# Graph attention pair: which engine forms and empties the pairwise differences in the statistics pass

## The reference

```python
D = jnp.abs(x[:, :, None, :] - x[:, None, :, :])
h = jnp.einsum('bijc,oc->bijo', D, W1) + b1
m = jnp.mean(h, axis=(0, 1, 2))
v = jnp.mean((h - m) ** 2, axis=(0, 1, 2))
h = (h - m) / jnp.sqrt(v + EPS) * g1 + be1
h = _leaky(h)
s = jnp.einsum('bijo,uo->biju', h, W2)[..., 0] + b2[0]
s = jnp.where(A_init > 0, s, NEG)
A = jax.nn.softmax(s, axis=-1)
y = jnp.einsum('bij,bjc->bic', A, x)
```

## Time and profile before

| | us |
|---|---|
| median of 3 runs | 2515.38 |
| lowest to highest | 2508.46 to 2524.46 |
| the profiled execution | 2519.5 |
| its span | 2517.8 |
| ScalarE busy | 2262.2 |
| VectorE busy | 2116.5 |
| TensorE busy (products) | 2052.3 |

### The profile page before, as it was taken

How to read it: one execution, slowest core, us unless ns; L and a number is a source line. 1 busy time by engine, 2 the same in 40 slices (tenths; PEclk the granted TensorE clock), 3 DMA queues, 4 the chain that set the end, 5 groups by cost and what they waited for, 6 DMA issues and landing times.

```text
span 2517.8 us, 36169 instructions
## 1 busy us (share of the span) xinstructions
PE 2052.3 (82%) x12997; PEld 837.5 (33%) x12997; DVE 2116.5 (84%) x2590; ACT 2262.2 (90%) x3505; POOL 61.7 (2%) x58
## 2 busy tenths in 40 slices
PE   4777766888888888888888888887888888888866
PEld 3555542323232322333232333231222222222236
DVE  4888866999999999999999999998878888788845
ACT  4999976999999999999999999996989899889965
POOL 0000000000000000000000000000000001000000
PEclk8999977999999999999999999998999999899978
DMA  3111113444444444444444444447988888888932
GB/s 112 39 44 40 39 47 125 179 161 171 177 173 166 167 171 178 172 170 176 165 172 171 173 171 168 170 162 272 330 308 320 314 314 316 292 314 320 336 114 67
DMA packets 230505, 470.52 MB, mean 187 GB/s; under 512 B 53496, under 2 KB 144312, under 8 KB 213944
## 3 DMA queue, kind: packets, MB, share of 16 engines
q1 hardware_dynamic: 229264, 467.84, 50.6%
q10 hardware_dynamic: 1064, 0.36, 0.1%
HBM read 254.19 MB, written 213.91 MB: 186 GB/s over the span
## 4 chain that ended last, share of the span: by engine, by line
ACT 25%; PE 24%; issue 17%; DVE 14%; DMA 11%; SPq 7%; POOL 2%; ACTq 0%; DVEq 0%; POOLq 0%
PE banks L899 11%; ACT banks L649 10%; DVE diff L1263 6%; DMA ring_scores<-sring 5%; ACT hcopy L646 5%; ACT habs L646 5%; DMA ub<-ring_scores 4%; DVE ring L1116 4%; PE banks L810 2%; SPq L441 2%; POOL ub L502 2%; ACT diff L634 2%; SPq L421 2%; DVE diff L1277 2%; PE banks L914 2%
## 5 line engine op out<-in xcount | busy, mean ns | idle before, releaser
L899 PE MATMUL banks<-diff,w1t 128*64 128x512 f32 x5136 | 1233.5, 611 | 192.8 <-ACT banks L649 142.1
L1263 DVE TENSOR_TENSOR diff<-ring 128x2048 f32<-128x2048 f32 x352 | 802.8, 2288 | 116.3 <-PE banks L899 116.3
L899 PEld LDWEIGHTS banks<-diff,w1t 128*64 128x64 f32 x5136 | 345.2, 138 | 938.7 <-issue 857.3
L649 ACT ACTIVATE banks<-banks,par 128x1024 f32<-128x1024 f32 x512 | 559.2, 1092 | 7.4 <-PE banks L899 4.8
L1277 DVE TENSOR_SCALAR diff<-diff 128x2048 int32<-128x2048 int32 x354 | 415.4, 1219 | 0.0
L1391 DVE TENSOR_TENSOR diff<-ring 128x2048 f32<-128x2048 f32 x128 | 292.7, 2287 | 47.6 <-PE banks L899 47.6
L634 ACT ACTIVATE diff<-banks 128x2048 f32<-128x2048 f32 x128 | 240.3, 1878 | 12.4 <-PE banks L914 12.4
L646 ACT ACTIVATE hcopy<-banks 128x1024 f32<-128x1024 f32 x192 | 197.0, 1026 | 18.4 <-PE banks L899 18.1
L646 ACT ACTIVATE habs<-banks 128x1024 f32<-128x1024 f32 x192 | 197.0, 1026 | 18.4 <-PE banks L899 18.1
L670 ACT ACTIVATE habs<-banks,par 128x1024 f32<-128x1024 f32 x128 | 153.4, 1198 | 46.6 <-PE banks L899 46.6
L914 PE MATMUL banks<-pick,yt 32*128 32x256 f32 x2560 | 184.8, 403 | 10.7 <-DMA yt<-xrows 10.7
(11 more groups left out here) (214 smaller groups left out, 1974.7 us busy)
## 6 DMA issues: line engine op xcount, KB each, us to landing
diff<-kept_two SPq DMA_DIRECT2D x86, 1024.0 KB, 6.8
kept_two<-hcopy SPq DMA_DIRECT2D x128, 512.0 KB, 2.6
kept_two<-habs SPq DMA_DIRECT2D x128, 512.0 KB, 2.6
hcopy<-kept_two SPq DMA_DIRECT2D x42, 1024.0 KB, 6.6
kept_one<-hcopy SPq DMA_DIRECT2D x64, 512.0 KB, 2.6
kept_one<-habs SPq DMA_DIRECT2D x64, 512.0 KB, 2.6
hcopy<-kept_one SPq DMA_DIRECT2D x64, 512.0 KB, 7.5
habs<-kept_one SPq DMA_DIRECT2D x64, 512.0 KB, 7.7
```

The costliest lines, as they stand in the source:

```text
L649: nc.scalar.activation(h, h, ACT.Square, bias=par[:, 53:54], accum_out=column(SQUARES + c)).then_inc(sq_done, 1)
L899: last = nc.tensor.matmul(dst[half * O:(half + 1) * O, bank * BANK:(bank + 1) * BANK], w1t[:, :], src[:, m * BANK:(m + 1) * BANK], start=T ...
L1263: v.tensor_tensor(shaped(diff[:, c % ND, :]), xj, xi_, ALU.subtract).then_inc(sub_done, 1)
```

## The change

All eight rectangle chunks of a graph are made by selection on TensorE. `ORDER` now puts them on the even places, and the diagonal chunks on the odd ones. The even places are emptied in turn: places 0, 4, 8, 12 by ScalarE (`abs_even`, with the sum), places 2, 6, 10, 14 by VectorE, which clears the sign bit while it reads `dps` and writes `diff` (`absolute_of_picked`, `abs_odd`). Selection r serves place 2r, is issued behind the projection of place 2r - 3, and waits for the emptying before. VectorE issues, per four places, the subtractions of 4q+1 and 4q+3, then the absolute values of 4q+1, 4q+2 (out of PSUM) and 4q+3. The x blocks per graph grow from 2 x 5 to 2 x 8. The second selection of the first graph stands before the first projection.

```diff
-    ORDER = [(0, 0), (4, 0), (4, 1), (1, 0), (5, 0), (5, 1), (2, 0), (6, 0), (6, 1), (3, 0), (7, 0), (7, 1),
-             (0, 1), (1, 1), (2, 1), (3, 1)]
-    ON_PE = [(0, 0), (1, 0), (2, 0), (3, 0), (0, 1)]
+    ORDER = [(0, 0), (4, 0), (0, 1), (4, 1), (1, 0), (5, 0), (1, 1), (5, 1),
+             (2, 0), (6, 0), (2, 1), (6, 1), (3, 0), (7, 0), (3, 1), (7, 1)]
-    NP, NR = len(ON_PE), len(REDONE)
+    NP, NR = 2 * RECTS, len(REDONE)
...
-            def absolute(b, j):
-
-                n = b * NP + pe_before(j)
-                act.wait_ge(pd_ready, n + 1)
-                if b or j >= ND:
+            def absolute(b, q):
+
+                j = 4 * q
+                act.wait_ge(pd_ready, b * NP + 2 * q + 1)
+                if b or q:
                     act.wait_ge(h_ready, in_order(b, j) - ND + 1)
...
+                nc.scalar.activation(diff[:, in_order(b, j) % ND, :], dps, ACT.Abs,
+                                     accum_out=column(EVENS + b * NR + q)).then_inc(abs_even, 1)
...
                     sum_h(b, j)
-                    if j + 3 in PE_AT:
-                        absolute(b, j + 3)
-                    if j + 3 == CHUNKS and b + 1 < B:
+                    if j % 4 == 1 and j + 3 < CHUNKS:
+                        absolute(b, (j + 3) // 4)
+                    elif j % 4 == 1 and b + 1 < B:
                         absolute(b + 1, 0)
...
-            def pick_differences(b, j):
+            def pick_differences(b, r):
+
+                k, tp = ORDER[2 * r]
+                if r == 0:
                     pe.wait_ge(blk_loaded[b % 2], 256 * (b // 2 + 1))
-                if n:
-                    pe.wait_ge(abs_pe, n)
-                e = 2 * pe_before(j)
+                if r % 2:
+                    pe.wait_ge(abs_even, b * RECTS + r // 2 + 1)
+                elif b or r:
+                    pe.wait_ge(abs_odd, b * RECTS + r // 2)
+                e = 2 * (RECTS * tp + k)
...
+            pick_differences(0, 1)
             pe.wait_ge(shift_ready, 1)
             for b in range(B):
                 for j in range(CHUNKS):
...
+                    if j % 4 == 0:
+                        pe.wait_ge(abs_even, b * RECTS + j // 4 + 1)
+                    elif j % 4 == 2:
+                        pe.wait_ge(abs_odd, b * RECTS + j // 4 + 1)
                     else:
-                        stat_chunk(in_order(b, j), False, b * (CHUNKS - NP) + dve_before(j) + 1)
-                    if j + 3 in PE_AT:
-                        pick_differences(b, j + 3)
-                    if j + 3 == CHUNKS and b + 1 < B:
-                        pick_differences(b + 1, 0)
+                        pe.wait_ge(abs_dve, b * PAIRS + j // 2 + 1)
+                    stat_chunk(in_order(b, j))
+                    if j % 2 and j + 3 < CHUNKS:
+                        pick_differences(b, (j + 3) // 2)
+                    elif j % 2 and b + 1 < B:
+                        pick_differences(b + 1, (j + 3 - CHUNKS) // 2)
...
+            def absolute_of_picked(b, q):
+
+                j = 4 * q + 2
+                dve.wait_ge(pd_ready, b * NP + 2 * q + 2)
+                if b or q:
+                    dve.wait_ge(h_ready, in_order(b, j) - ND + 1)
+                v.tensor_scalar(diff[:, in_order(b, j) % ND, :].bitcast(I32), dps.bitcast(I32), ABS_BITS, None,
+                                ALU.bitwise_and).then_inc(abs_odd, 1)
...
             for b in range(B):
-                if b:
-                    differences_between(b, 1, 3)
-                differences_between(b, 4, 6)
-                differences_between(b, 7, 9)
-                differences_between(b, 10, 12)
-                differences_between(b, 13, 16)
+                for q in range(RECTS):
+                    z = b * PAIRS + 2 * q + 1
+                    subtract(b, 4 * q + 1)
+                    subtract(b, 4 * q + 3)
+                    absolute(in_order(b, 4 * q + 1), z)
...
+                    absolute_of_picked(b, q)
+                    absolute(in_order(b, 4 * q + 3), z + 1)
```

More of the change, by code:

```diff
@@ L48, in gnn_pair_kernel @@
     BLK = 16
-    ORDER = [(0, 0), (4, 0), (4, 1), (1, 0), (5, 0), (5, 1), (2, 0), (6, 0), (6, 1), (3, 0), (7, 0), (7, 1),
-             (0, 1), (1, 1), (2, 1), (3, 1)]
-    ON_PE = [(0, 0), (1, 0), (2, 0), (3, 0), (0, 1)]
+    ORDER = [(0, 0), (4, 0), (0, 1), (4, 1), (1, 0), (5, 0), (1, 1), (5, 1),
+             (2, 0), (6, 0), (2, 1), (6, 1), (3, 0), (7, 0), (3, 1), (7, 1)]
     REDONE = [(0, 0), (1, 0), (2, 0), (3, 0)]
-    NP, NR = len(ON_PE), len(REDONE)
+    NP, NR = 2 * RECTS, len(REDONE)
     NK = CHUNKS - NR
     KB = 8
-    PE_AT = [j for j, c in enumerate(ORDER) if c in ON_PE]
     STEPS = (0, 4, 1, 5, 2, 6, 3, 7)
@@ L229, in gnn_pair_kernel @@
         pd_ready = sem("pd_ready")
-        abs_pe = sem("abs_pe")
+        abs_even = sem("abs_even")
+        abs_odd = sem("abs_odd")
         abs_dve = sem("abs_dve")
@@ L309, in kept_before @@
             return sum(c not in REDONE for c in ORDER[:j])
[L311 to L317, removed]
         block = ctx.enter_context(nc.Block())
@@ L901, in project @@
                 return last
-            def pick_differences(b, j):
-                n = b * NP + pe_before(j)
-                if pe_before(j) == 0:
+            def pick_differences(b, r):
+                k, tp = ORDER[2 * r]
+                if r == 0:
                     pe.wait_ge(blk_loaded[b % 2], 256 * (b // 2 + 1))
-                if n:
-                    pe.wait_ge(abs_pe, n)
-                e = 2 * pe_before(j)
+                if r % 2:
[3 more added lines that the diff above has]
+                e = 2 * (RECTS * tp + k)
                 for s in range(2):
@@ L917, in pick_differences, with stat_chunk @@
                 last.then_inc(pd_ready, 1)
-            def stat_chunk(c, by_pe, count):
-                pe.wait_ge(abs_pe if by_pe else abs_dve, count)
+            def stat_chunk(c):
                 if c >= 2:
@@ L932, in _ @@
                 for j in range(CHUNKS):
-                    if j in PE_AT:
-                        stat_chunk(in_order(b, j), True, b * NP + pe_before(j) + 1)
-                    else:
-                        stat_chunk(in_order(b, j), False, b * (CHUNKS - NP) + dve_before(j) + 1)
-                    if j + 3 in PE_AT:
-                        pick_differences(b, j + 3)
-                    if j + 3 == CHUNKS and b + 1 < B:
-                        pick_differences(b + 1, 0)
+                    if j % 4 == 0:
+                        pe.wait_ge(abs_even, b * RECTS + j // 4 + 1)
+                    elif j % 4 == 2:
+                        pe.wait_ge(abs_odd, b * RECTS + j // 4 + 1)
+                    else:
+                        pe.wait_ge(abs_dve, b * PAIRS + j // 2 + 1)
[4 more added lines that the diff above has]
+                        pick_differences(b + 1, (j + 3 - CHUNKS) // 2)
             for j in range(2):
-                stat_chunk(B * CHUNKS + j, False, B * (CHUNKS - NP) + j + 1)
+                pe.wait_ge(abs_dve, B * PAIRS + j + 1)
+                stat_chunk(B * CHUNKS + j)
             pe.wait_ge(st_small, 2)
@@ L1295, in _ @@
                 v.tensor_copy(agg[:, 1, half * O:(half + 1) * O], w1t[:, :])
[L1296 to L1301, removed]
-            for b in range(B):
-                if b:
-                    differences_between(b, 1, 3)
-                differences_between(b, 4, 6)
-                differences_between(b, 7, 9)
-                differences_between(b, 10, 12)
-                differences_between(b, 13, 16)
+            for b in range(B):
+                for q in range(RECTS):
[3 more added lines that the diff above has]
+                    absolute(in_order(b, 4 * q + 1), z)
+                    if b == 0 and q == 0:
+                        dve.wait_ge(abs_even, 1)
+                        v.tensor_scalar(par[:, 52:53], yt[:, SUMS + EVENS:SUMS + EVENS + 1], -1.0 / CH, None,
+                                        ALU.mult).then_inc(shift_sum, 1)
+                        dve.wait_ge(shift_half, 1)
+                        v.tensor_copy(par[:, 53:54], ps[3][:, 0:1]).then_inc(shift_ready, 1)
+                    absolute_of_picked(b, q)
+                    absolute(in_order(b, 4 * q + 3), z + 1)
             for j in range(2):
@@ L1311, in _ @@
             for j in range(2):
-                absolute(B * CHUNKS + j, B * (CHUNKS - NP) + j + 1)
+                absolute(B * CHUNKS + j, B * PAIRS + j + 1)
             for j in range(2):
```

## The result

The changed kernel takes 2553.34 us (median of 4 runs, 2533.09 to 2558.84) against 2514.86 us before (median of 4 runs). The medians lie 1.5% apart; the ratio of the means of the runs is 1.0135, 95% interval 1.0081 to 1.0189. It is slower. Its profiled execution takes 2553.16 us with a span of 2551.4 us, 33.6 us more than before.

A forecast was written before the change was run, and what follows sets the result against it. It took waits around ScalarE and TensorE, not summed busy time, to bound the pass. Profiled 2519.5 + 29.8 for rounds + 1 for first loads = 2550.3, so a median of about 2546 us, range 2528 to 2568.

The forecast's parts named there:

- The likeliest case: Statistics pass: VectorE and ScalarE rounds of four chunks both above the present 10.20 us; 2546 us, chance 0.66.
- The VectorE ring: Four-chunk round of waits through VectorE and TensorE, with the PSUM operation counting fully: 10.43 us, the longer one.
- The ScalarE ring: Four-chunk round from projection 4q+1 through ScalarE's copies, Squares and Abs to the release of projection 4q+5: 10.38 us.
- the round of three chunks: Kernel before, one selected chunk in three: a chain of waits around ScalarE and TensorE sets the pace, 7.29 us.
- The price out of PSUM: VectorE's absolute value of 2048 columns read from PSUM: 2.27 us, between 1.22 and 2.26 from scaled copies.
- Nothing gets in each other's way: Denies the rival that VectorE's PSUM reads crowd ScalarE and TensorE, or the clock drops: 2588 us at 2.6 us; chance 0.08.
- The freed ScalarE time: Rival: one Abs less on ScalarE, 1.86 us a graph, comes back whole, giving 2457 us; chance 0.06.
- +29.8 us for the rounds: Statistics pass: four rounds of 10.43 make 41.72 us a graph, +0.93 over 40.79, times 32 graphs.
- 1 us for the first loads: First graph's bigger x block loads on SP delay TensorE: 1 us taken, between nothing and 4.1.
- the tail of the pass: Two half chunks behind the last projection keep their order, so no time was added.
- The start: Wait for the first graph's x loads, 64 KB for 40: 1 us added, at most 4.1.
- Three rings: Rounds of 10.43 (VectorE) and 10.38 (ScalarE), plus a path through projection 4q+4 with cover 0.43 us.

The follow-up runs named there:

- e5: Changed kernel plus an extra 1024-column VectorE read of PSUM ahead of each absolute value out of PSUM: round 11.59 us, against 10.46; device time 2693.8 us.
- e1: Changed kernel with VectorE's subtraction 4q+3 moved behind the absolute value out of PSUM: round 10.39 us, against 10.46; device time 2540.6 us.
- e4: Changed kernel with the absolute value out of PSUM over 1024 of 2048 columns in 31 graphs: round 10.39 us, against 10.46; device time 2534.1 us.
- e2: Changed kernel without ScalarE's keep copy of place 4q+3 in 31 of 32 graphs: round 10.46 us, as before the edit; device time 2538.8 us.
- e6: Kernel before the change, with each subtraction at places 13 to 15 followed at once by its absolute value: 2479.68 us against 2520.45, ratio 0.9846.
- e9: Changed kernel with all eight selected chunks taken out of PSUM by ScalarE, none by VectorE: round 11.03 us, against 10.46; device time 2617.5 us.
- e3: Changed kernel with subtraction 4q+3 moved later and the keep copy of place 4q+3 left out in 31 graphs: round 10.01 us; device time 2497.4 us.
- e8: Like e3, but the keep copy left out in 31 graphs is that of place 4q+1: round 9.39 us, against 10.01; device time 2422.8 us.

## Why the prediction was right

- **The time.** 2546 us was predicted, 2553 measured: +1.2% against +1.5% between the medians (+1.35% between the means). The likeliest case came, two rings above the present pace.
- **The VectorE ring.** Predicted 10.43, measured 10.46 us. Step by step: subtraction 2.21 and 2.20, to the operation out of PSUM 1.13 and 1.14, to the selection 2.32 and 2.34, to the projection 1.08, to the next 1.71, to the subtraction 1.98 and 1.99. e5 shows that it sets the pace: 1.13 us more in one of its steps make the round 1.13 us longer.
- **The ScalarE ring.** Predicted 10.38, 10.37 in the trace of the changed kernel, 10.39 as the round of e1 and e4, where it is the longest. That it takes over is shown by e1 and e4, and by e2 that it isn't the first.
- **What bounded the kernel before.** Here the prediction claimed more than its rows show. It called the round of three chunks, 7.29 us, a pass around ScalarE and TensorE and "not a sum of busy time". But over three such rounds of the kernel before ScalarE is busy 21.82 of 21.88 us (columns as in the earlier trace rows). The only step of ScalarE's that is longer than usual is from the Square at 1031.17 to the one at 1032.41, for which the ring's projection at 1030.44 is needed: 1.24 us, where a Square otherwise takes 1.09. So the ring lies 0.15 us above ScalarE's own steps, 7.29 against 7.14 us:

```profile
1017.72:1039.60 21.88, 19.79 (x123) 7.06 (x121) 20.05 (x12) 21.82 (x37) 0.00 (x0) 1.00 0.46 175
...
1031.17 1.10 ACT L649 ACTIVATE banks<-banks,par 128x1024 f32<-128x1024 f32 x1
```

  Nearly all of ScalarE's idle time before, 1.13 of 1.23 us a graph, lay in the last four chunks, and e6 removed it. The forecast rests on the two new rings and the measured 40.79 us, so this doesn't touch its number.
- **The price out of PSUM.** Predicted 2.27, measured 2.283 us for 2048 columns; e5 has 1.22 us for 1024. From 1024 to 2048 columns it grows by 1.04 ns a column, in SBUF the whole 2048 take 1.22 us. The Trainium skill (VectorE: DVE Perf Modes, Why PSUM operands drop a tier) says that an fp32 operand in PSUM is read at the lowest rate only. The trace agrees: out of PSUM the same operation takes 1.87 times as long as in SBUF (2283 and 1218 ns).
- **Nothing gets in each other's way.** The subtraction takes 2288 ns as before, the Abs 1877 ns (1878), the Square 1097 ns (1092), and the clock is 1.00. That rival fell.
- **The freed ScalarE time.** It didn't come back: 1.65 us a graph less busy (39.56 and 37.91), and 1.14 us a graph more time, so that ScalarE is idle 4.02 us a graph after 1.23. In e2 another 1.0 us a round off ScalarE left the round as it was. The Trainium skill (Perfetto Trace Analysis, Identifying the Most-Contended Engine) says to optimize the engine of the highest occupancy first; at 97% before, that was ScalarE. These runs bear it out in part. Taking work off ScalarE made the kernel slower, since the new order brought longer waits; taking its wait away (e6) made it faster, and from e9, where ScalarE is busy all the time, to the changed kernel, which has less work on it, the round falls by 0.57 us.
- **The sum, where it was small.** Predicted +29.8 us for the rounds and 1 us for the first loads, measured +38.1 us in the pass and nothing for the loads, so the 29.8 us are 8.3 us short. Four rounds took 4 x 0.03 more, 3.8 us in 32 graphs. One wait was not costed: once a graph the selection comes 0.09 us later behind VectorE, 2.9 us in all. In the timeline of TensorE's selections in the changed kernel these are two of even rank, the first in the middle of a graph, the other the first of a graph:

```profile
1016.40 1.15 PE L904 MATMUL banks<-pick,yt 32*128 32x256 f32 x16 [0.26 <-DVE diff L1279]
...
1026.95 1.15 PE L904 MATMUL banks<-pick,yt 32*128 32x256 f32 x16 [0.35 <-DVE diff L1279]
```

  The code has one more wait there, for the x blocks, which had long been loaded. I read the 0.09 us as the price of that second wait; it was not tried alone. These two terms are 6.7 us. Another 1.1 us lie in the tail of the pass, which the prediction put at nothing since it keeps its order: from the last graph's first selection to the half-chunk statistics it is 48.7 us before (1662.02 to 1710.7), 7.9 more than a graph, and 50.9 us after (1697.88 to 1748.8), 9.0 more than a graph. The last 0.5 us lie in the first graphs.
- **The start.** I took 1 us for bigger first loads. The loads of 64 KB take 0.43 us to issue as those of 40 KB did, and the first selection starts at 396.52 us: nothing. The changed kernel's line answers to the first load line of the earlier trace rows:

```profile
L358 SPq DMA_DIRECT2D yt<-xrows x256: 303/431/1700, 387.1 to 1671.1; - x128
```

## What to carry to other kernels

An engine at 97% busy leaves 3% to be won from its waits, and a new order that takes work off it can lose more than that in new ones. Follow one steady round from start to start through the queues, add up every ring that closes, and take the longest; shortening it gains only down to the next one. Before work is moved between engines, look whether moving an instruction within its own queue takes a wait away: here three subtractions, each followed at once by its absolute value, gave 1.5%, and the whole redistribution cost 1.35%. Steps read from the old trace priced the new order to 0.03 us in 10.4.

## What the runs showed that I had not expected

- Three rings lay within 0.45 us of each other (10.46, 10.37, 10.01 us). That is why a microsecond taken off one place gave 0 or 0.07 us, and the same microsecond 0.62 us more at another (e3 and e8).
- A second wait on TensorE's queue that had long been met went with 0.09 us more between VectorE's end and the selection in the changed kernel and in e2 and e5, where TensorE stands waiting there. In e1 and e8, where that selection waits for nobody, the round that holds it is no longer than the others (10.39 and 9.39 us).
- ScalarE was busy 39.56 us a graph before, and 39.56 us is what a graph takes in e6: one wait in a graph was nearly all the idle time that it had.
- A load's issue on SP stayed at 0.43 us as its size went from 40 to 64 KB.
